# Feed-forward: one of VectorE's passes goes to GpSimd, with a third buffer and a changed order on three engines

## What is computed

```python
def float2fix(x, mantissa_bits):
    s = jnp.float32(2.0 ** mantissa_bits)
    q = jnp.round(x * s) / s
    return x + jax.lax.stop_gradient(q - x)

def pwlin_gelu_basic(x, mantissa_bits_in, mantissa_bits_out):
    xq = float2fix(x, mantissa_bits_in)
    y = jnp.interp(xq, _PWL_X, _PWL_Y)          # 33 points of exact GELU on [-4, 4]
    y = jnp.where(xq > 4.0, xq, jnp.where(xq < -4.0, jnp.float32(0.0), y))
    return float2fix(y, mantissa_bits_out)

h = jnp.einsum('bsd,df->bsf', x, w1) + b1       # x: layer norm of x + attention
h = float2fix(h, 8)
h = pwlin_gelu_basic(h, 8, 8)
h = float2fix(h, 8)
out = jnp.einsum('bsf,fd->bsd', h, w2) + b2
return float2fix(out, 8)
```

## Time and profile before

| | us |
|---|---|
| median of 3 runs | 261.66 (259.95 to 262.92) |
| the profiled execution: time | 259.94 |
| the profiled execution: first to last instruction (span) | 258.1 |
| mean granted TensorE clock | 0.934 of full speed |
| VectorE busy | 219.8 |
| TensorE busy | 190.2 |
| ScalarE busy | 149.1 |
| GpSimd busy | 98.0 |
| feed-forward groups, L787 of (0,0) to the end | 153.93 to 258.1 |

### The profile page before, as it was taken

The page is one execution under the profiler, slowest core; times in us unless marked ns, Lnnn a source line. Parts: engine busy times, 40 slices in busy tenths (PEclk is TensorE's granted clock), DMA queues, the critical chain, the costliest instruction groups (busy, mean ns, idle before and its releaser), DMA issues.

```text
span 258.1 us, 8513 instructions
## 1 busy us (share of the span) xinstructions
PE 190.2 (74%) x3227; PEld 147.2 (57%) x3227; DVE 219.8 (85%) x497; ACT 149.1 (58%) x227; POOL 98.0 (38%) x177
## 2 busy tenths in 40 slices
PE   1268878879778788787887895947869697694753
PEld 0247767667667576666675542727565655463642
DVE  6877989889898898988897399999797989999951
ACT  1023677757676567766666768561929284856401
POOL 4456757776668676677754220000000000000000
PEclk9997799999999999999999998885979799979879
DMA  4411111011110011000000000001010101010111
GB/s 113 143 44 41 44 43 32 20 40 41 41 41 22 19 41 41 20 20 3 3 3 3 6 0 1 0 0 43 0 41 0 41 0 44 0 41 0 41 42 42
DMA packets 14488, 7.47 MB, mean 29 GB/s; under 512 B 1017, under 2 KB 14335, under 8 KB 14466
## 3 DMA queue, kind: packets, MB, share of 16 engines
q1 hardware_dynamic: 14050, 6.97, 9.4%
q10 hardware_dynamic: 416, 0.20, 0.3%
HBM read 5.06 MB, written 2.10 MB: 28 GB/s over the span
## 4 chain that ended last, share of the span: by engine, by line
DVE 38%; PE 23%; issue 14%; ACT 10%; POOL 9%; DMA 3%; DVEq 1%; SPq 0%; POOLq 0%; ACTq 0%
PE bank_o L1054 6%; DVE y_raw L795 5%; DVE g_hi L787 5%; DVE xn_all L579 4%; ACT g_hi L491 4%; PE bank_o L944 3%; DVE v_blk L623 3%; DVE parts L608 3%; DVE frac L780 2%; PE g_hi L887 2%; DVE act_q L806 2%; ACT hz L475 2%; PE banks_s L1039 2%; DVE partsT L615 2%; PE g_hi L914 2%
## 5 line engine op out<-in xcount | busy, mean ns | idle before, releaser
L1054 PEld LDWEIGHTS bank_o<-w,act_q 128*128 128x128 f32 x256 | 38.2, 230 | 4.0 <-issue 3.6
L420 ACT ACTIVATE probs<-banks_s 128x512 f32<-128x512 f32 x64 | 34.5, 599 | 10.0 <-PE banks_s L928 9.9
L1054 PE MATMUL bank_o<-w,act_q 128*128 128x128 f32 x256 | 38.1, 314 | 0.0
L1039 PE MATMUL banks_s<-x2T,w 128*128 128x512 f32 x60 | 32.7, 629 | 0.0
L321 POOL TENSOR_TENSOR parts<-qk_hat,parts 128x256 f16<-128x256 f32 x32 | 22.8, 731 | 11.1 <-DVE parts L603 11.1
L944 PE MATMUL bank_o<-probs,v_blk 128*32 128x64 f32 x1024 | 20.7, 221 | 7.5 <-DVE attn L637 7.5
L491 ACT ACTIVATE g_hi<-seg,gelu_hi 128x1024 f32<-128x1024 f32 x16 | 17.9, 1118 | 11.6 <-DVE y_raw L795 11.6
L944 PEld LDWEIGHTS bank_o<-probs,v_blk 128*32 128x32 f32 x1024 | 16.1, 109 | 11.3 <-issue 8.3
L863 PE MATMUL bank_o<-b_parts,ones 128*128 128x512 f16 x8 | 4.0, 501 | 24.4 <-DVE x_all L812 24.4
L329 POOL TENSOR_TENSOR x_all<-x_all,attn 128x256 f32 (+1 forms) x16 | 11.7, 729 | 24.7 <-DVE attn L637 24.7
L914 PE MATMUL g_hi<-ident,parts 128*128 128x128 f16 x256 | 20.2, 223 | 1.0 <-POOL parts L321 0.6
(11 more groups left out here) (105 smaller groups left out, 473.0 us busy)
## 6 DMA issues: line engine op xcount, KB each, us to landing
x_all<-in_x_dram SPq DMA_DIRECT2D x16, 128.0 KB, 2.3
c_in<-in_ctx_dram SPq DMA_DIRECT2D x16, 128.0 KB, 2.1
out_dram<-x_all SPq DMA_DIRECT2D x8, 256.0 KB, 2.3
w<-in_L_ffn_w_dram SPq DMA_DIRECT2D x2, 256.0 KB
wkv_raw<-in_L_xattn_Wkv_dram ACTq DMA_DIRECT2D x1, 128.0 KB, 3.2
bkv_rep<-in_L_xattn_bkv_dram SPq DMA_DIRECT2D x1, 128.0 KB
wq_raw<-in_L_xattn_Wq_dram ACTq DMA_DIRECT2D x1, 64.0 KB, 2.3
b_rows<-in_L_xattn_bq_dram SPq DMA_DIRECT2D x1, 1.5 KB
```

The source lines that it names most:

```text
L420: a.activation(probs[i][:].rearrange("p t g n -> p (t g n)"), bank_s(i), ACT.Exp).then_inc(S["probs_ready"], 1)
L1039: last = t_.matmul(out, w1[:, f0:f0 + P], x2T[gr % 2][:], start=False, stop=True)
L1054: last = t_.matmul(out, act_q[u][:, c, P * t:P * t + P], w2[:, CH // UNITS * u + c, :], start=False, stop=(u == UNITS - 1 and t == GT - 1 ...
```

## The change

The sum g_lo + y_raw (f_interpolate) of 15 of the 16 units moves from VectorE to GpSimd; the last unit's stays on VectorE. g_lo gets three buffers, by n modulo 3, instead of one for each u. On VectorE f_round moves one unit later than it was: the round of a unit comes behind the next unit's product. ScalarE's low table pass and its rounding of the hidden units come a unit further ahead. TensorE issues the second half of a group's `down` at the start of the next group, and the transposes ahead of down(gr, 0).

```diff
--- before.py
+++ after.py
@@ -158,7 +158,7 @@
         hz = [sb(f"hz{u}", [P, UW]) for u in range(UNITS)]
         seg0 = [sb(f"seg0{u}", [P, UW]) for u in range(UNITS)]
         frac = [sb(f"frac{u}", [P, UW], I32) for u in range(UNITS)]
-        g_lo = [sb(f"g_lo{u}", [P, UW]) for u in range(UNITS)]
+        g_lo = [sb(f"g_lo{k}", [P, UW]) for k in range(3)]
         y_raw = [sb(f"y_raw{u}", [P, UW]) for u in range(UNITS)]
         act_q = [sb(f"act_q{u}", [P, UW // GTOK, GTOK]) for u in range(UNITS)]
 
@@ -371,10 +371,20 @@
                 step(s)
 
 
+            def f_interpolate(gr, u):
+
+                n = UNITS * gr + u
+                wait(pool, "slope_done", n + 1)
+                g.tensor_tensor(y_raw[u][:], g_lo[n % 3][:], y_raw[u][:], ALU.add).then_inc(S[f"gelu{u}_done"], 1)
+
             step(STEPS - 1)
             rstd_x2(STEPS - 2)
             residual(STEPS - 1)
             rstd_x2(STEPS - 1)
+            for gr in range(GROUPS - 1):
+                f_interpolate(gr, 0)
+                f_interpolate(gr, 1)
+            f_interpolate(GROUPS - 1, 0)
 
 
         @block.scalar
@@ -478,8 +488,9 @@
 
                 n = UNITS * gr + u
                 wait(act, "seg_ready", n + 1)
-                wait(act, f"gelu{u}_done", gr)
-                a.activation(g_lo[u][:], seg0[u][:], ACT.Gelu, bias=gelu_lo[:], scale=1.0 / FIX).then_inc(S["glo_ready"], 1)
+                if n >= 3:
+                    wait(act, f"gelu{(n - 3) % 2}_done", (n - 3) // 2 + 1)
+                a.activation(g_lo[n % 3][:], seg0[u][:], ACT.Gelu, bias=gelu_lo[:], scale=1.0 / FIX).then_inc(S["glo_ready"], 1)
 
             def gelu_high(gr, u):
 
@@ -495,18 +506,22 @@
                 wait(act, "ff_proj", gr + 1)
                 a.activation(bank_o[:], bank_o[:], ACT.Identity, bias=round_out[:]).then_inc(S["ffr_ready"], 1)
 
+            def unit(stage, n):
+
+                if n < UNITS * GROUPS:
+                    stage(n // UNITS, n % UNITS)
+
             def group(gr):
-                gelu_low(gr, 1)
-                if gr + 1 < GROUPS:
-                    round_hidden(gr + 1, 0)
-                gelu_high(gr, 1)
-                if gr + 1 < GROUPS:
-                    gelu_low(gr + 1, 0)
-                    round_hidden(gr + 1, 1)
+
+                n = UNITS * gr
+                unit(gelu_high, n + 1)
+                unit(gelu_low, n + 2)
+                unit(round_hidden, n + 3)
                 if gr >= 1:
                     round_out_ff(gr - 1)
-                if gr + 1 < GROUPS:
-                    gelu_high(gr + 1, 0)
+                unit(gelu_high, n + 2)
+                unit(gelu_low, n + 3)
+                unit(round_hidden, n + 4)
                 if gr + 3 < GROUPS:
                     copy_x2(gr + 3)
 
@@ -533,6 +548,8 @@
             gelu_low(0, 0)
             gelu_high(0, 0)
             copy_x2(2)
+            gelu_low(0, 1)
+            round_hidden(1, 0)
             for gr in range(GROUPS):
                 group(gr)
             round_out_ff(GROUPS - 1)
@@ -771,6 +788,7 @@
                 n = UNITS * gr + u
                 wait(dve, "hz_ready", n + 1)
                 wait(dve, "ghi_ready", n - 1)
+                wait(dve, "glo_ready", n - 1)
                 v.tensor_scalar(seg0[u][:].bitcast(I32), hz[u][:].bitcast(I32), -SEG, None, ALU.bitwise_and).then_inc(S["seg_ready"], 1)
 
             def f_fraction(gr, u):
@@ -784,7 +802,7 @@
                 n = UNITS * gr + u
                 wait(dve, "ghi_ready", n + 1)
                 wait(dve, "glo_ready", n + 1)
-                v.tensor_tensor(g_hi[:], g_hi[:], g_lo[u][:], ALU.subtract).then_inc(S["rise_ready"], 1)
+                v.tensor_tensor(g_hi[:], g_hi[:], g_lo[n % 3][:], ALU.subtract).then_inc(S["rise_ready"], 1)
 
             def f_slope(gr, u):
 
@@ -794,11 +812,6 @@
                 wait(dve, f"actq{u}_ready", gr)
                 v.scalar_tensor_tensor(y_raw[u][:], g_hi[:], 1.0 / SEG, frac[u][:], ALU.mult, ALU.mult).then_inc(S["slope_done"], 1)
 
-            def f_interpolate(gr, u):
-
-                wait(dve, "slope_done", UNITS * gr + u + 1)
-                v.tensor_tensor(y_raw[u][:], g_lo[u][:], y_raw[u][:], ALU.add).then_inc(S[f"gelu{u}_done"], 1)
-
             def f_round(gr, u):
 
                 wait(dve, f"gelu{u}_done", gr + 1)
@@ -814,23 +827,20 @@
             def group(gr):
                 f_rise(gr, 0)
                 f_slope(gr, 0)
-                f_interpolate(gr, 0)
+                if gr >= 1:
+                    f_round(gr - 1, 1)
                 if gr + 1 < GROUPS:
                     f_segment(gr + 1, 0)
-                f_round(gr, 0)
-                if gr + 1 < GROUPS:
                     f_fraction(gr + 1, 0)
                 if gr == 0:
                     norm_x2(STEPS - 1)
                 f_rise(gr, 1)
                 f_slope(gr, 1)
-                f_interpolate(gr, 1)
                 if gr >= 1:
                     f_out(gr - 1)
+                f_round(gr, 0)
                 if gr + 1 < GROUPS:
                     f_segment(gr + 1, 1)
-                f_round(gr, 1)
-                if gr + 1 < GROUPS:
                     f_fraction(gr + 1, 1)
 
 
@@ -845,7 +855,11 @@
             for gr in range(GROUPS):
                 group(gr)
 
-            f_out(GROUPS - 1)
+            last = GROUPS - 1
+            dve.wait_ge(S["slope_done"], UNITS * GROUPS)
+            v.tensor_tensor(y_raw[1][:], g_lo[(UNITS * GROUPS - 1) % 3][:], y_raw[1][:], ALU.add).then_inc(S["gelu1_done"], 1)
+            f_round(last, 1)
+            f_out(last)
 
 
         @block.tensor
@@ -1056,14 +1070,15 @@
                 last.then_inc(S[("actq0_used", "ff_proj")[u]], 1)
 
             def group(gr):
+                if gr >= 1:
+                    down(gr - 1, 1)
                 if gr + 2 < GROUPS:
                     hidden(gr + 2, 0)
-                down(gr, 0)
                 if gr + 3 < GROUPS:
                     transpose_x2(gr + 3)
+                down(gr, 0)
                 if gr + 2 < GROUPS:
                     hidden(gr + 2, 1)
-                down(gr, 1)
 
             def hidden_first(c):
 
@@ -1099,6 +1114,7 @@
             transpose_x2(2)
             for gr in range(GROUPS):
                 group(gr)
+            down(GROUPS - 1, 1)
 
 
 # ---- launch: one core; inputs and outputs as the reference has them ----
```

## The result

The changed kernel takes 263.38 us (median of 20 runs), the kernel before 261.52 (20 runs): a ratio of 1.0075, interval 1.0047 to 1.0103. It is slower by 0.5 to 1.0%, less than the 1.1% (264.6 us) forecast. The profiled execution has a span of 262.4 us.

A forecast was written before the change was run, and what follows sets the result against it. It took VectorE's instruction stream to bound the feed-forward. Start +0.8, six groups +3.4, last group -0.7 and -0.7, wait slots 0.1 gave +2.9 us: 264.6 us against the 261.66 median, 1.1% more, range 257.0 to 271.5.

The forecast's parts named there:

- The bound: Feed-forward: VectorE's instruction stream sets the time, 11.5 us a group without gaps; six groups take 73.68 us.
- The sum on GpSimd: The moved 1024-wide add takes 2.35 us on GpSimd, with ends of 1.87 and 2.92.
- F + 2.83: End of GpSimd's add after unit 0, counted from F, the start of the VectorE instruction that follows the product.
- The conflict: VectorE's SBUF-to-SBUF passes stand until GpSimd's add ends: 2.08 us lost after unit 0, 1.77 after unit 1, each group.
- Rival 1: VectorE keeps the shared path through its back-to-back fast passes; the add falls under rise and product: 249.9 us, chance 0.10.
- Rival 2: No conflict between GpSimd's add and VectorE at this size; some 10 us a group, 245.3 us, chance 0.05.
- rival 3: GpSimd's add is shorter, 1.87 us: 6.7 us less, 257.9 us, chance 0.07.
- rival 4: GpSimd's add is longer, 2.92 us: 8 us more, 272.6 us, chance 0.08.
- rival 5: TensorE is late with down by more than the 1.8 us covered; 1 us late gives 270.6, chance 0.04.
- Waits taken away by TensorE's order: Segment pass's waits for ScalarE in the feed-forward, 0.75 us a group, end with the new order, which costs nothing.
- The sum: Total over the profiled execution: start +0.8, six groups +3.4, last group -0.7 and -0.7, wait slots 0.1, together +2.9 us.
- the end behind the last product: Last group: f_out starts 1.26 us earlier, the last 32 products (5.01 us) start 0.60 later; together -0.7 us.

The follow-up runs named there:

- experiment 1: The changed kernel with all 16 sums back on VectorE, its order and three g_lo buffers kept: 257.56 us, ratio 0.983.
- experiment 7: The kernel before with TensorE's new order alone: 257.40 us, ratio 0.981.
- experiment 2: The changed kernel with one more wait on GpSimd, so each sum also waits for the fraction pass after its product: 246.28 us, ratio 0.942.
- experiment 3: The changed kernel with GpSimd's sum over 512 of the 1024 columns, the other half left out: 251.54 us in one run, beside 261.9 of before.
- experiment 5: The kernel before with a useless 128x1024 add on GpSimd, released by each product: 277.48 us in one run, beside 262.36 of before.
- experiment 6: The kernel before with a useless GpSimd add, released by the fraction pass that follows the product: 264.75 us in one run, beside 262.2 of before.
- experiment 4: The kernel before with four unused 128x512 products on TensorE ahead of the last group's 32 products: 259.85 us, ratio 0.9945.

## Why the prediction was right

The forecast was 1.1% slower; measured 0.75%, in the range and the right way. By its steps:

- **The bound** was VectorE's instruction stream. Experiments 1 and 7 bring every group behind the first to its 11.53 us once the waits are gone.
- **The sum on GpSimd**, 2.35 us forecast, takes 2.34 where it has nothing to wait for, 2.73 after unit 0, where a round goes ahead of it (2.66 by the forecast's F + 2.83). The estimate from the page of the Trainium skill (GPSIMD Engine Reference, "Elementwise — side-by-side cycle accounting"), 2.25, was 4% short: half of a time for 2048 elements leaves out that a part of it is not per element.
- **The conflict** came pass by pass as put: segment 2.84 (forecast 2.77), round 2.46 (2.46), half groups 6.36 and 6.57 (6.28 and 6.57), a group 12.93 (12.85). Experiments 2, 3 and 5 show its nature: it disappears where GpSimd works beside passes that read PSUM, it follows the length of GpSimd's instruction, and it needs no dependence. The rule of the Trainium skill (SBUF — State Buffer, "Who interferes with whom"), a pair of ports held for a whole instruction, agrees with all three, and its further statement that a pass with two SBUF inputs shares them with a GpSimd instruction that reads SBUF agrees with experiments 5 and 6 (2.87 against 1.89 us).
- **Rival 1** (VectorE keeps the path through its run of fast passes) needed the segment pass at 0.69 behind the first round; it took 2.84. **Rival 2** fell with it, **rivals 3 and 4** with the 2.34 us, **rival 5** since f_out waited for nothing but at the very end.
- **Waits taken away by TensorE's order**: as forecast, and experiment 7 puts them on TensorE's order alone. The price of the added semaphore wait, a guess of 0.05 us that the forecast reckons at 0.3 in one place and 0.1 in another, doesn't show: a group takes 11.53 us with it (experiment 1) and without (experiment 7).
- **The sum**: the start came out at 14.10 us from first rise to the product of (1,0), against 13.24 before: +0.86 (forecast +0.8). Six groups take 77.61 against 73.68: +3.9 (+3.4). The second rise of the last group is as forecast, -0.7.
- **The term that was mis-sized** is the end behind the last product: forecast -0.7, measured 262.4 - 251.55 against 258.1 - 245.24, -2.0. The forecast kept the 5.01 us of the last 32 products; they took 3.73 (experiment 4). With it the sum would have been +1.6; half a microsecond too little in the groups makes up the rest to 2.1. So two errors of opposite sign, 1.3 too much at the end and some 0.6 too little in start and groups, made the total closer than its worst term. That the low clock had passed before the last products began is not in the forecast, and in that part its nearness is luck.

## What to carry to other kernels

In this kernel, moving an elementwise pass from VectorE to GpSimd cost time where GpSimd's instruction met passes from SBUF to SBUF, and paid where it ran beside VectorE passes that read PSUM. So sort VectorE's passes into those that share a path with GpSimd's instruction and those that don't, and release GpSimd's work at the start of a run of the second kind, even if its data are ready earlier. Here a single added wait turned 0.75% slower into 5.8% faster (TensorE's order alone gives 1.9% of it). And a pass that is blocked counts as busy and shows in no table of waits: compare the duration of one form across its places.

## What the runs showed of the hardware

- A GpSimd add of 128x1024 f32 takes 2.34 us with two different input tiles (2.37 beside rise and product in experiment 2), and 1.89 with the same tile as both inputs (experiment 6).
- GpSimd gets its turn between two VectorE passes that follow each other without a gap, also where these are 1024 wide; a VectorE pass of 128x1024 that was held up ends 0.55 us behind GpSimd's instruction, whether that takes 1.26, 2.34 or 2.87 us.
- A VectorE pass with two SBUF inputs holds GpSimd's add up, from 1.89 to 2.87 us (experiments 5 and 6).
- TensorE's last 32 products took 3.73 to 6.42 us over the ten profiles, with a granted clock of 1.00 to 0.56 over their length; length times clock is 3.6 to 3.8 us in each. The idleness just ahead of them was 0 to 7.57 us and gives no order: 3.73 us after 0, 1.62 and 2.31, but 6.42, 5.31 and 5.36 after 2.17, 6.07 after 3.88, 5.01 after 4.94, 5.57 after 5.21 and 5.40 after 7.57. What decides it stays open; unused products in the gap gave the full clock in both kernels in which they were tried.
